# A decoder layer on one core: probabilities turned earlier, a copy of the queries moved to VectorE, an epsilon moved into the squares

## The reference

```python
x = x + gla(_layernorm(x))
x = x + xattn(_layernorm(x), ctx_1024)
x = x + ffn(_layernorm(x))          # top 2 of 4 experts, 512 tokens each

def gla(x):                         # per head
    S = S * exp(g)[..., None] + k[..., None] * v[..., None, :]   # over time
    o = einsum('bhk,bhkv->bhv', q, S)
    o = (o - o.mean(-1)) * rsqrt(o.var(-1) + 1e-5)               # per head
    return silu(x @ Wg.T + bg) * o @ Wo.T

def xattn(x, y):                    # y: 112 main rows, 16 rows of their own softmax
    q = ln(x @ Wq + bq, qn_w, qn_b)     # per head, epsilon 1e-6
    k = ln(y_main @ Wk + bk, kn_w, kn_b); v = y_main @ Wv + bv
    ctx = softmax(q k / sqrt(32)) v + (the same for the last 16 rows, their own weights)
    return ctx @ Wo + bo
```

## Time and profile before

| what | value |
|---|---|
| median of 3 runs | 957.51 us (956.81 to 957.78) |
| the profiled execution | 955.95 us, its span 954.2 us |
| PE busy over the span | 888.2 us (93%) |
| DVE, ACT, POOL busy | 676.3, 447.0, 474.0 us |
| first step of scores in turn 3, in turn 15 | 111.56 us, 475.64 us |

### The profile page before, as it was taken

How to read it: one execution, slowest core, us unless ns; L and a number is a source line. 1 busy time by engine, 2 the same in 40 slices (tenths; PEclk the granted TensorE clock), 3 DMA queues, 4 the chain that set the end, 5 groups by cost and what they waited for, 6 DMA issues and landing times.

```text
span 954.2 us, 19601 instructions
## 1 busy us (share of the span) xinstructions
PE 888.2 (93%) x7588; PEld 508.9 (53%) x7588; DVE 676.3 (71%) x1313; ACT 447.0 (47%) x748; POOL 474.0 (50%) x532
## 2 busy tenths in 40 slices
PE   3787999999999999999999888999999999999995
PEld 1545666666666666666665644444444444444442
DVE  6997888888888888888886749665562564445952
ACT  3654665666657665666656633222331342223210
POOL 1666877788777878778773310120720010005833
PEclk9899999999999999999999999999999999999999
DMA  7614000000000000000022035232462443236693
GB/s 270 198 56 141 4 20 18 21 3 19 19 16 19 3 19 17 18 19 3 19 68 92 12 130 205 86 98 83 130 177 89 133 143 121 95 124 210 173 258 109
DMA packets 42414, 81.89 MB, mean 86 GB/s; under 512 B 11778, under 2 KB 12098, under 8 KB 42370
## 3 DMA queue, kind: packets, MB, share of 16 engines
q1 hardware_dynamic: 37378, 66.58, 21.3%
q0 software_dynamic: 4992, 14.70, 5.7%
HBM read 67.62 MB, written 13.65 MB: 85 GB/s over the span
## 4 chain that ended last, share of the span: by engine, by line
PE 51%; POOL 23%; DVE 11%; issue 7%; ACT 4%; DMA 1%; POOLq 1%; SPq 0%; DVEq 0%; ACTq 0%
PE ps L1198 15%; PE ps L1200 15%; PE ps L1199 15%; POOL hrs L677 6%; POOL pr L737 4%; PE ps L1204 2%; POOL hrs L675 2%; POOL rstd L662 2%; POOL dk L693 1%; PE ps L1420 1%; POOL kraw L719 1%; DVE wl L1725 1%; POOL od L711 1%; POOL pr L739 1%; POOL gate L705 1%
## 5 line engine op out<-in xcount | busy, mean ns | idle before, releaser
L1171 ACT ACTIVATE big<-ps 128x512 f32<-128x512 f32 x64 | 38.2, 596 | 202.7 <-PE ps L1200 202.7
L1198 PE MATMUL ps<-big,w1h 128*128 128x512 f16 x256 | 97.0, 379 | 0.8 <-DVE big L1725 0.8
L1199 PE MATMUL ps<-big,w1h 128*128 128x512 f16 x256 | 97.0, 379 | 0.0
L1200 PE MATMUL ps<-big,w1l 128*128 128x512 f16 x256 | 97.0, 379 | 0.0
L1200 PE MATMUL ps<-w2h,h_more 128*128 128x512 f16 x256 | 97.0, 379 | 0.0
L833 POOL DMA_INDIRECT y_fetched<-y_scratch,idx_get x32 | 40.0, 1250 | 96.8 <-DMA y_scratch<-big 87.4
L816 POOL DMA_INDIRECT big<-x_scratch,token_of x16 | 18.5, 1155 | 137.5 <-PE ps L1204 77.5
L677 POOL TENSOR_TENSOR hrs<-hvar,neg_half 128x16 f32<-128x16 f32 x28 | 80.9, 2906 | 0.0
L1199 PE MATMUL ps<-w2l,big 128*128 128x512 f16 x176 | 66.7, 379 | 0.0
L1198 PE MATMUL ps<-w2h,big 128*128 128x512 f16 x176 | 66.7, 379 | 0.0
L737 POOL TENSOR_TENSOR pr<-pr,rc 128x896 f32<-128x896 f32 x31 | 52.2, 1685 | 17.7 <-DVE rc L1943 17.7
(11 more groups left out here) (354 smaller groups left out, 2485.9 us busy)
## 6 DMA issues: line engine op xcount, KB each, us to landing
wst<-in_w SPq DMA_DIRECT2D x28, 1024.0 KB, 5.3
x_scratch<-xn SPq DMA_DIRECT2D x16, 256.0 KB, 2.1
y_fetched<-in_w SPq DMA_DIRECT2D x4, 1024.0 KB, 14.5
out<-x_all SPq DMA_DIRECT2D x4, 1024.0 KB, 7.3
pr<-in_w_attn SPq DMA_DIRECT2D x3, 1024.0 KB, 8.3
x_all<-in_w_attn SPq DMA_DIRECT2D x3, 1024.0 KB, 11.5
x_all<-in_x SPq DMA_DIRECT2D x1, 3072.0 KB, 11.4
y_scratch<-big SPq DMA_DIRECT2D x12, 256.0 KB, 4.3
```

Of the source, the lines that this page charges most:

```text
L1171: act.activation(hg[f % NH], H_PS[f % NH], ACT.Gelu, scale=UN).then_inc(hg_r, 1)
L1198: nc.tensor.matmul(o, lh, rh, start=first, stop=False)
L1199: nc.tensor.matmul(o, lh, rl, start=False, stop=False)
L1200: return nc.tensor.matmul(o, ll, rh, start=False, stop=last)
```

## The change

There are three edits.

1. On PE the fourth group of probabilities is turned before the keys, and their product with the values comes before the decay gate's first product. On ACT the copy of that gate's product goes behind the copy of the context.
2. In the pipeline's body the copy of the turned queries goes from ACT (`q_out`, with the activation's scale and bias) to DVE (`b1_q_out`, a tensor_scalar, multiply and add), behind the context's low half. The drain keeps it on ACT.
3. The recurrent squares go to a tile of their own with an epsilon column. The tile `hsq` has 34 columns per head: the recurrent squares with epsilon in column 0 (`osq`, columns 0 to 32), the squares of the keys with epsilon in column 33 (`ksq`, columns 1 to 33). POOL's addition is gone.

```diff
+        hsq = sb("hsq", [P, HEADS, DV + 2])
+        osq, ksq = hsq[:, :, 0:DV + 1], hsq[:, :, 1:DV + 2]
@@ gpsimd
+            pool.memset(osq[:, :, 0:1], DV * EPS_HEAD[0])
-                if n == 0:
-                    pool.tensor_tensor(hve[:, :], hvar[0][:, :], eps_head[:, 0, :], ALU.add).then_inc(hdev[0], 1)
-                    after(pool, hdev[0], b, nth=1, per=2)
-                    pool.tensor_tensor(hrs[0][:, :], hve[:, :], neg_half[:, :], ALU.pow).then_inc(hdev[0], 1)
-                else:
-                    pool.tensor_tensor(hrs[n][:, :], hvar[n][:, :], neg_half[:, :], ALU.pow).then_inc(hdev[n], 2)
+                pool.tensor_tensor(hrs[n][:, :], hvar[n][:, :], neg_half[:, :], ALU.pow).then_inc(hdev[n], 2)
@@ scalar
-                square(od[:, :], b1, o_ps, s[0], hq[0])
+                square(osq[:, :, 1:DV + 1], heads(b1), o_ps, s[0], hq[0])
@@ scalar, body
-                on(s[0], kg1_out)
                 on(s[2], k_out)
                 on(s[3], c_hi)
+                on(s[0], kg1_out)
                 on(s[1], o_square)
-                on(s[2], q_out)
@@ tensor, body
                 on(s[3], b2_turn, 2)
+                on(s[3], b2_turn, 3)
                 on(s[2], b1_kT)
-                on(s[3], b2_turn, 3)
+                on(s[3], b2_pv)
                 on(s[0], a1_kg1)
-                on(s[3], b2_pv)
@@ vector
+            def b1_q_out(s):
+                after(dve, qT_ps, s[0])
+                dve.tensor_scalar(qT[:, :, :], cols(c0), head_cols[:, 0:1], head_cols[:, 1:2], ALU.mult, ALU.add).then_inc(qT_r, 1)
@@ vector, body
                 on(s[3], b2_low)
-                on(s[1], head_var, 0, od)
+                on(s[2], b1_q_out)
+                on(s[1], head_var, 0, osq)
```

More of the change, by code:

```diff
@@ L124, in decoder_layer @@
         hvar = [sb(f"hvar{n}", [P, HEADS]) for n in range(3)]
-        hve = sb("hve", [P, HEADS])
         hrs = [sb(f"hrs{n}", [P, HEADS]) for n in range(3)]
@@ L132, in decoder_layer @@
         eps_row = sb("eps_row", [P, 3])
-        eps_head = sb("eps_head", [P, 3, HEADS])
         one_col = sb("one_col", [P, 1])
@@ L163, in decoder_layer @@
         vx = [sb(f"vx{i}", [P, D]) for i in range(2)]
-        ksq = sb("ksq", [P, HEADS, DV + 1])
+        hsq = sb("hsq", [P, HEADS, DV + 2])
+        osq, ksq = hsq[:, :, 0:DV + 1], hsq[:, :, 1:DV + 2]
         kT = sb("kT", [P, KC, L])
@@ L640, in _ @@
                 pool.memset(eps_row[:, n:n + 1], EPS_ROW)
-                pool.memset(eps_head[:, n, :], DV * EPS_HEAD[n])
             pool.memset(one_col[:, :], 1.0)
@@ L1067, in head_deviation @@
                 after(act, hv[n], s[0])
-                act.activation(hln[n][:, :], hvar[n][:, :], ACT.Ln, bias=eps_head[:, 0, 0:1] if n == 0 else 0.0).then_inc(hdev[n], 1)
+                act.activation(hln[n][:, :], hvar[n][:, :], ACT.Ln, bias=0.0).then_inc(hdev[n], 1)
                 after(act, hdev[n], s[0], nth=1, per=2)
@@ L1795, in head_var @@
                 after(dve, hq[n], s[0])
-                dve.tensor_reduce(hvar[n][:, :], sq[:, :, :] if n else heads(sq[:, :]), AX.X, ALU.add).then_inc(hv[n], 1)
+                dve.tensor_reduce(hvar[n][:, :], sq[:, :, :], AX.X, ALU.add).then_inc(hv[n], 1)
             def head_norm(s, n, dst, src, done, scale=1.0):
@@ L1997, in refined @@
                 after(dve, hdev[n], s[0], nth=2, per=2)
-                chained(dve.scalar_tensor_tensor(newton[n][:, :], hvar[n][:, :], 0.0 if n else DV * EPS_HEAD[0], hrs[n][:, :], ALU.add, ALU.mult))
+                chained(dve.scalar_tensor_tensor(newton[n][:, :], hvar[n][:, :], 0.0, hrs[n][:, :], ALU.add, ALU.mult))
                 chained(dve.scalar_tensor_tensor(newton[n][:, :], newton[n][:, :], -0.5, hrs[n][:, :], ALU.mult, ALU.mult))
@@ L2024, in drain @@
                 b2_low(p)
-                head_var(r, 0, od)
+                head_var(r, 0, osq)
                 refined(r, 0)
```

## The result

| | before | after |
|---|---|---|
| median, runs side by side | 958.06 us (956.81 to 962.2, 13 runs) | 954.98 us (953.21 to 958.3, 13 runs) |
| ratio, 95% interval | | 0.9964 [0.9954, 0.9974] |
| span of the profiled execution | 954.2 us | 951.1 us |
| pitch of the scores, turn 3 to 15 | 30.34 us | (471.22 - 110.28) / 12 = 30.08 us |

The change makes the kernel faster by about 0.36%, 3.4 us by the ratio (the two medians differ by 3.1). The forecast was 4.4 us. The time lies in the range and the sign is right, but every term behind it is off.

A forecast was written before the change was run, and what follows sets the result against it. PE, busy 93%, was taken as the bound, its recurring gaps winnable only up to POOL's chain; 13 turns x (0.32 + 0.09) = 5.3 less 0.9 of ramp gave 4.4 us, so 953.1 us, range 951 to 955.4.

The forecast's parts named there:

- Edit 1: Reordering on PE and ACT: the queries' turn on PE starts 0.32 us earlier per turn, bounds 0.17 and 0.43.
- T: Start of PE's turn of the queries in a loop turn, from which later times are measured.
- floor: Earliest start of PE's queries' turn, set by POOL's powers and DVE's scaling: at most 0.43 us earlier a turn.
- first rival: All gaps close: 0.43 plus 0.09 us a turn and no ramp cost, 6.8 us gained, 950.7 us; chance 18%.
- Edit 2, the copy: Queries' copy moved from ACT to DVE takes 0.68 instead of 0.77 us, so the scores start 0.09 earlier a turn.
- What stands behind the copy: Recurrent squares' sum on DVE starts 0.42 later, POOL's power saves 0.38; gated output just fits, at worst 0.05 a turn.
- second rival: Recurrent norm's chain replaces the wait, POOL held by DVE: gain 0.08 a turn, 957.4 us, no change; chance 15%.
- The ramp: In turn 2 the sum, DVE's weight split and POOL's held power move 0.89 later: costs 0.9 us, bounds 0.5 and 1.1.
- The sum: 13 turns x (0.32 + 0.09) = 5.3 us, less 0.9 for turn 2, gives 4.4 us gained.
- third rival: Slower: the recurrent norm's chain with a longer DVE copy, priced at 1.01 us, gives 962 us; chance 9%.

The follow-up runs named there:

- e1: The kernel before with only the reordered PE and ACT steps (edit 1): 950.10 us, ratio 0.9943.
- e5: The changed kernel with constants 1 and 0 instead of the two columns in DVE's copy of the queries: 955.04 us in a single run.
- e7: Edits 1 and 3, with the queries turned into two banks and copied half on ACT, half on DVE: 950.06 us, ratio 0.9941 to the kernel before.
- e6: The changed kernel without edit 3, so POOL's addition stays: 957.98 us in a single run.
- e4: The changed kernel with the copy of the queries left on ACT (edits 1 and 3): 948.83 us, ratio 0.9926; again 949.51 us, 0.9925.
- e3: The kernel before with edit 3 alone (epsilon column, no addition on POOL): 954.94 us, ratio 0.9985.
- e9: The changed kernel, but in turn 2 only ACT copies the queries: 952.11 us, ratio 0.9954.

## Why the prediction was right, and where its terms failed

**Edit 1: right in sign and inside its bounds, but bound by something else.** 0.32 a turn was forecast between 0.17 and 0.43; e1 shows 0.40. The forecast had ACT's copies set T, with only 0.17 in the even turns. The traces have the floor in every turn: PE turns the queries 0.06 behind DVE's scaling of them, where it was 0.47. That part of the first rival came true, and the 0.43 that the prediction had as the most was nearly the value. The overlap of ACT's two copies (1.08 instead of 1.20) helped to reach it.

**Edit 2, the copy: wrong in sign.** "I take 0.68: 0.09 earlier." With constants it would have been so (0.69 and 0.08 in e5). The nearest row had constants as its scalars, and its operand form was the difference. The copy takes 0.81, and the scores start 0.04 later against T than from ACT. My upper bound, "0.77 or a little over", was the right end. The Trainium skill's page "VectorE: DVE Perf Modes" had the direction right in the rule that I set aside (section "Specifications": ScalarE closer to PSUM), as the copy takes 0.81 on DVE and 0.77 on ACT here; my estimate of 0.66 us for DVE from its table is not what this form takes.

**What stands behind the copy: wrong.** "It just fits. I count nothing for it, at worst 0.05 a turn." The working gave T + 7.61 and the trace T + 7.84, and PE turns it at T + 7.97:

- The sum starts at 230.42, T + 1.42, which is 0.54 later than before and not 0.42: 0.12 of the copy. This part moves the scores as well, and so costs PE nothing more at the gated output (e5).
- Without POOL's addition the power starts 231.26 - 230.42 = 0.84 behind the sum's start, where it was 233.40 - 232.27 = 1.13: 0.29 saved, not 0.38.
- PE starts 0.13 behind POOL's end (236.84 to 236.97), where the forecast had nothing and the second rival 0.06. That is so in turns 4 to 15, the loop. In turn 3, which is written out, it is 0.05 (below), and PE turns the gated output only 6.33 behind the scores. What takes the other 0.08 in the loop is not shown.

POOL, then PE, in turn 3 after:

```profile
115.30 1.27 POOL L705 TENSOR_TENSOR od<-od,gate 128x512 f32<-128x512 f32 x1
```

```profile
116.62 0.66 PE L1197 MATMUL ps<-ident,od 128*128 128x128 f32 x4
```

In e1, where nothing is late, PE turns the gated output 234.68 - 228.38 = 6.30 behind the scores; here it is 6.41, so 0.11 is lost. The profile shows no idle time for it: the matmul before starts at 236.64 and is shown 0.38 long, past the start at 236.97, though the matmuls before that one started every 0.22. The sum over a steady turn closes: 0.40 - 0.04 - 0.11 = 0.25 against the measured 0.26. The same sum gives e7 (29.94 - 0.21 + 0.09 = 29.82, measured 29.82).

**The ramp: wrong, as two effects that I had joined.** The delay is there: e6, with POOL's addition, has the gated output 1.05 later than before (10.30 against 9.25), where I forecast 0.9. But "It moves with the split by 0.89, although its addition is gone" is the step that failed. Without the addition the power starts 0.07 ahead of DVE's split instead of 0.24 behind it, and takes 2.92 instead of 4.84. DVE, then POOL, in turn 2 after, against the earlier trace rows:

```profile
78.49 2.31 DVE L1718 SCALAR_TENSOR_TENSOR wl<-x_all,wh 128x2048 f16<-128x2048 f32 x1
```

```profile
78.42 2.92 POOL L671 TENSOR_TENSOR hrs<-hvar,neg_half 128x16 f32<-128x16 f32 x1 [1.80 <-DVE hvar L1789]
```

So PE's turn of the gated output comes 1.14 earlier than in e6, more than the 1.05 that e6 was late, and PE's wait in turn 2 fell from 3.89 to 3.73 instead of growing to 4.8. The power itself ends 2.2 earlier than in e6. The rest is not won because another chain takes over, DVE's own queue: its scaling of the recurrent output stands behind the split, the maximum and the subtraction. DVE, then POOL:

```profile
83.24 0.68 DVE L1793 SCALAR_TENSOR_TENSOR od<-ps,hrs 128x512 f32<-128x512 f32 x1
...
84.29 1.52 DVE L1823 TENSOR_TENSOR_SCAN G<-carry,lsg 128x256 f32<-128x256 f32 x1
```

```profile
84.00 1.27 POOL L705 TENSOR_TENSOR od<-od,gate 128x512 f32<-128x512 f32 x1 [1.42 <-DVE od L1793]
```

**The sum.** Forecast 13 x 0.41 - 0.9 = 4.4. From the scores of turn 3 to those of turn 15 there are 12 pitches: 12 x 0.41 = 4.9 was forecast, 12 x 0.26 = 3.1 is shown. The stretch from T of turn 2 to the scores of turn 3 holds the thirteenth gain and the ramp's cost, so it should have grown by 0.5. It shrank by 0.8 in the first profile and grew by 0.5 in the second, whose low stretch there is twice as long. The forecast was near by luck: an error of 1.8 us in the steady turns met one of up to 1.3 the other way in turn 2, and inside the steady turns edit 1's 0.08 too little met the copy and its chain. Of edit 1's 0.40 a turn, 0.04 went to the longer copy (the third rival's condition) and 0.11 to the norm's chain (the second rival's place, for other reasons), together over a third.

**Where 3.4 us more were.** In the profiles, edit 2 costs 12 x 0.145 = 1.7 in the steady turns and 2.1 to 3.3 in turn 2. The drain is 1.4 shorter with it, as e1 and both profiles of e4 lost 1.71 of clock at 526 to 532 and the change did not. Together that is 2.4 to 3.6, and 3.4 was measured. Why the drain has that fall was not found. The copy of the queries is on ACT in the body of before and e3 too, and they have none; nor has e9, with the same idle times of 0.96 and 0.39 ahead of the place.

## What to carry to other kernels

When a copy moves to another engine, price it by a row with the same operand form (constants or columns), and list what stood first in the queue that it joins: here the sum of squares, whose chain had 0.24 us of room, less the 0.13 that PE takes to start behind POOL in the loop. Compare starts, not idle times, where matmuls are pipelined: both the 0.11 lost and the floor that edit 1 ran into show no idle time on PE. Where a change has a part that pays for another (edit 3 for edit 2), ask what the first part (edit 1) would give alone: it gave more than the whole. An idle gap on TensorE and a stretch of low clock did not add up here: a low stretch ahead of a gap is partly hidden in it, and one behind it is paid.

## What the runs showed of the hardware

- A DVE tensor_scalar from PSUM, 128x512 f32, takes 0.69 us with constants (e5) and 0.80 to 0.81 with two columns. ACT does the same with scale and bias columns in 0.77.
- POOL's power of 16 columns takes 2.92 us when it starts 0.07 before DVE's 2.31 us split of weights (both inputs in SBUF), and 4.84 when it starts 0.24 behind the split's start. In turn 2 of all 13 profiles it is one or the other, by whether the addition stands ahead of it. The split takes 2.31 either way. Started 0.15 before the end of DVE's 0.38 us pass (231.26 against 231.41) the power takes 2.92 as well. The other way round, DVE's scan G takes 0.69 alone (237.15 in turn 7 after) and 1.52 when it starts at 84.29, 0.29 into POOL's multiplication of 1.27. The rule of contention that I had quoted from the Trainium skill ("GPSIMD Engine Reference", section "1. Specifications") is borne out where one of the two starts well inside a long operation of the other, and not by the split beside a power that started first.
- From 34 us to the router the granted clock fell in stretches at one half that lost 1.71 or 3.41 us each: at 34 to 43, 66 to 74 and 76 to 95 us, and in e1 and e4 at 526 to 532. Between 95 and 526 us it was 1.00 in every profile. Two profiles of the same kernel can differ by one stretch or by its length.
